# A two-layer decoder on one core: the 16-head weighted sums of its first and last stage on four quarters of the array, norms of the last stage by Ln and Exp, and new orders of both stages

## What is computed

```
x = x + L0_attn(ln(x))          # stage A: delta-rule attention, 4 heads of 32
x = x + L0_xattn(ln(x), ctx)    # stage B: causal attention on ctx, 16 heads of 8
x = x + L0_ffn(ln(x))           # stage C: 6 layers of local attention (16 heads of 64) and GELU MLP
x = x + L1_attn(ln(x))          # stage D: causal attention, q and k of unit length, 16 heads of 8
x = x + L1_xattn(ln(x), ctx)    # stage E: gated attention on ctx, 8 heads of 16
x = x + L1_ffn(ln(x))           # stage F: 16 experts, 3 chosen per token, all computed
```

## Time and profile before

| | us |
|---|---|
| median of 3 runs | 4253.59 (4252.46 to 4254.8) |
| the profiled execution's own time | 4263.92 |
| its span, first to last instruction | 4262.1 |
| TensorE busy | 4071.3 (96% of the span) |
| ScalarE busy | 3488.6 (82%) |
| VectorE busy | 3291.7 (77%) |
| GpSimd busy | 2653.4 (62%) |

### The profile page before, as it was taken

One profiled execution on the slowest core, in us unless ns is written; L12 is line 12 of the kernel. 1 busy time (PEld: TensorE's weight loads), 2 busy tenths in 40 slices (PEclk: granted clock), 3 DMA queues, 4 the chain that ended last, 5 costly groups with the idle time before them and its releaser, 6 DMA issues.

```text
span 4262.1 us, 149492 instructions
## 1 busy us (share of the span) xinstructions
PE 4071.3 (96%) x61520; PEld 3074.8 (72%) x61520; DVE 3291.7 (77%) x9529; ACT 3488.6 (82%) x10059; POOL 2653.4 (62%) x2246
## 2 busy tenths in 40 slices
PE   7999989999999999999999999999999799999999
PEld 5777756666667666667666666676666588888889
DVE  4666578998888888888888888888888467767765
ACT  3455569999999999999999999999999356666665
POOL 3444467887777777777777777777777233333331
PEclk8888889999999999999999999999999789999999
DMA  3000000000000000000000000000000100000000
GB/s 105 4 4 4 4 2 4 5 4 5 30 3 4 4 30 4 4 4 4 30 4 5 5 30 4 5 3 9 27 10 9 30 2 4 4 4 4 4 4 7
DMA packets 65248, 46.34 MB, mean 11 GB/s; under 512 B 29220, under 2 KB 63032, under 8 KB 63800
## 3 DMA queue, kind: packets, MB, share of 16 engines
q1 hardware_dynamic: 64568, 36.78, 3.0%
HBM read 28.48 MB, written 2.10 MB: 7 GB/s over the span
## 4 chain that ended last, share of the span: by engine, by line
PE 41%; ACT 34%; DVE 8%; issue 2%; POOL 0%; ACTq 0%
PE ps L569 34%; ACT BIG L921 15%; ACT BIG L913 12%; PE ps L573 7%; DVE BIG L1149 3%; ACT ps L913 3%; ACT L928 2%; DVE sm L1160 2%; DVE BIG L1154 1%; ACT sm L921 1%; DVE BIG L1157 1%; DVE y_sb L1154 0%; DVE BIG L1153 0%; ACT XS L913 0%; POOL BIG L1591 0%
## 5 line engine op out<-in xcount | busy, mean ns | idle before, releaser
L569 PE MATMUL ps<-WB,BIG 128*128 128x128 f32 (+2 forms) x8576 | 1940.8, 363 | 53.4 <-DVE BIG L1157 47.7
L913 ACT ACTIVATE BIG<-ps 128x512 f32<-128x512 f32 (+6 forms) x3168 | 1518.4, 536 | 461.6 <-PE ps L573 277.8
L1591 POOL TENSOR_TENSOR BIG<-BIG,sm 128x512 f32<-128x512 f32 (+1 forms) x864 | 1221.3, 1425 | 563.6 <-DVE sm L1342 330.0
L569 PEld LDWEIGHTS ps<-WB,BIG 128*128 128x128 f32 (+1 forms) x8576 | 1154.3, 192 | 378.8 <-issue 224.7
L1591 POOL TENSOR_TENSOR BIG<-BIG 128x512 f32<-128x512 f32 x768 | 969.4, 1279 | 146.5 <-DVE BIG L1149 146.5
L1160 DVE TENSOR_REDUCE sm<-BIG 128x8 f32<-128x512 f32 (+3 forms) x1472 | 871.3, 610 | 157.8 <-ACT BIG L921 154.6
L573 PEld LDWEIGHTS ps<-t_ident,BIG 128*128 128x128 f32 x6016 | 731.3, 146 | 325.8 <-issue 167.8
L573 PE MATMUL ps<-t_ident,BIG 128*128 128x128 f32 x6016 | 888.0, 282 | 68.3 <-DVE BIG L1149 28.9
L569 PEld LDWEIGHTS ps<-BIG 64*64 64x64 f32 (+2 forms) x37888 | 617.4, 132 | 336.6 <-ACT BIG L913 78.3
L569 PE MATMUL ps<-BIG 64*64 64x64 f32 (+4 forms) x37888 | 737.2, 226 | 52.7 <-ACT BIG L913 18.6
L1594 POOL TENSOR_TENSOR sm<-sm,halfn 128x1 f32<-128x1 f32 (+2 forms) x336 | 290.5, 871 | 752.0 <-DVE sm L1153 419.8
(11 more groups left out here) (119 smaller groups left out, 2913.7 us busy)
## 6 DMA issues: line engine op xcount, KB each, us to landing
WB<-in_Wqkv SPq DMA_DIRECT2D x6, 1536.0 KB, 7.3
XS<-y_sb SPq DMA_DIRECT2D x96, 63.0 KB
y_sb<-in_ctx SPq DMA_DIRECT2D x16, 256.0 KB, 3.2
WB<-in_Wo SPq DMA_DIRECT2D x6, 512.0 KB, 9.0
x_sb<-in_x SPq DMA_DIRECT2D x8, 256.0 KB, 5.2
WB<-in_F_W SPq DMA_DIRECT2D x1, 2048.0 KB, 8.7
WB<-in_F_W SPq DMA_DIRECT2D x8, 256.0 KB, 4.9
out<-x_sb SPq DMA_DIRECT2D x8, 256.0 KB, 2.3
```

Source lines behind the costliest of these rows:

```text
L569: return te.matmul(o, l, r, start=start, stop=stop, skip_group_check=not check)
L913: return se.activation(o, i, ACT.Copy)
L1591: return pe_.tensor_tensor(o, a, b, op)
```

## The change

1. `weighted16` goes over j = 0 to 7 and does heads j and 8 + j together. Heads 0 to 7 (n = 0) go to one bank on the two diagonal quarters, heads 8 to 15 (n = 1) to the next bank on the other two, so that four consecutive matmuls use the four quarters. The two sequences of heads 8 to 15 thus come out in exchanged rows. The number and the shapes of the matmuls are as before.
2. Phase `u` takes a pair of banks. DVE `r` and `n` read both in one instruction each (`weighted`).
3. ACT `t` puts the rows right (`restore`): three copies of 64x128, 64x64 and 64x64 in the place of one of 128x128.
4. In stage D, `n1` to `n8` go; ACT phases `ln` and `lx` of 128x32 come in (Ln, then Exp with scale -0.5), as stage C has them. `n0` becomes one `max`. The constant `magic` goes.
5. All lists of `AB_ORDER` and `DE_ORDER` are new, and so are `SLOT` and `BEGIN`. `C_ORDER` stays. Some conditions on the reuse of banks and buffers are written out (`act D` for G, `dve a` for J, `act h` beside `act k`), since the orders no longer imply them.

```
 AB_ORDER = {
-    "pe": "V3 b12 s4 O3 u5 a22 o3 b22 T1 w3 a32 b32 G1 a42 D1 b42 v4 x3 X0 p14 t5 q3 Z2 a11 W2 y5 p04 J0",
+    "pe": "X1 q4 y6 v5 W3 a12 J1 V3 s4 b12 p05 a22 O3 b22 u5 a32 T1 o3 b32 w3 G1 a42 D1 b42 t5 p14 x3 Z2",
...
-SLOT = {"ab": 14.8, "c": 11.25, "de": 25.4}
+SLOT = {"ab": 12.999, "c": 11.246, "de": 24.357}
 BEGIN = {
-    "ab": {"pe": -0.7, "act": -3.5, "dve": -10.8, "pool": -18.7},
-    "c": {"pe": 482.5, "act": 484.2, "dve": 473.3, "pool": 463.2},
-    "de": {"pe": 3239.8, "act": 3223.5, "dve": 3222.9, "pool": 3321.6},
+    "ab": {"pe": 0.0, "act": -19.09, "dve": -26.15, "pool": -23.17},
+    "c": {"pe": 428.13, "act": 426.37, "dve": 418.35, "pool": 408.78},
+    "de": {"pe": 3171.62, "act": 3143.0, "dve": 3143.34, "pool": 3118.64},
...
-AB_PAIRS = ("G", "s")
+AB_PAIRS = ("G", "s", "u")
...
-DE_PAIRS = ("s", "G")
+DE_PAIRS = ("s", "G", "u")
...
+        def weighted(u):
+
+            return PS[u.bank["u"] // 2][:, :].rearrange("p (n c) -> p n c", n=2)[:, :, 0:72].rearrange("p n (h d) -> p n h d", d=9)
...
-            def weighted16(K, PT, V):
-                for h in range(16):
-                    c = 128 * (h % 4) + 64 * (h // 4 % 2)
-                    for q in (slice(0, 64), slice(64, 128)):
-                        o = mm(K[q, 9 * h:9 * h + 9], PT[h // 8][q, c:c + 64], V[q, 9 * h:9 * h + 9])
+            def weighted16(k, PT, V):
+
+                for j in range(8):
+                    c = 128 * (j % 4) + 64 * (j // 4)
+                    for n in range(2):
+                        for bb in range(2):
+                            q, r, v = slice(64 * bb, 64 * bb + 64), slice(64 * (bb ^ n), 64 * (bb ^ n) + 64), 72 * n + 9 * j
+                            o = mm(bank[k + n][r, 9 * j:9 * j + 9], PT[n][q, c:c + 64], V[q, v:v + 9])
                 return o
...
+            def restore(o, K):
+
+                copy(o[0:64, :], K[0:64, 0:128])
+                copy(o[64:128, 0:64], K[64:128, 64:128])
+                return copy(o[64:128, 64:128], K[64:128, 0:64])
...
+                elif ph == "ln":
+                    w.wait_ge(*u.on("dve", "n0"))
+                    o = act(sm[:, 5, 0:32], sm[:, 2, 0:32], ACT.Ln)
+                elif ph == "lx":
+                    w.wait_ge(*u.on("act", "ln"))
+                    o = act(sm[:, 5, 0:32], sm[:, 5, 0:32], ACT.Exp, scale=-0.5)
...
-                    o = stt(sm[:, 2, 0:32], sm[:, 1, 0:32], 1e-16, sm[:, 1, 0:32], ALU.max, ALU.max)
-                elif ph[0] == "n" and len(ph) > 1:
-                    o = newton(u, sm[:, 5, 0:32], sm[:, 2, 0:32], sm[:, 6, 0:32], int(ph[1:]) - 1)
+                    o = ts(sm[:, 2, 0:32], sm[:, 1, 0:32], 1e-16, None, ALU.max)
```

More of the change, by code:

```diff
@@ L158 @@
 for _x in EXPERTS:
-    DE_EMPTIED.update({"h" + _x: ("act k" + _x,), "o" + _x: ("dve x" + _x,)})
-DE_PAIRS = ("s", "G")
+    DE_EMPTIED.update({"h" + _x: ("act h" + _x, "act k" + _x), "o" + _x: ("dve x" + _x,)})
+DE_PAIRS = ("s", "G", "u")
 class Unit:
@@ L239, in build @@
         halfn = sb("halfn", [128, 8])
-        magic = sb("magic", [128, 32], U32)
         woA = sb("woA", [128, 128])
@@ L674, in pe_ab @@
                         w.wait_ge(*u.on("act", m))
-                    o = weighted16(K, b.PT, b.V9)
+                    o = weighted16(u.bank[ph], b.PT, b.V9)
                 elif ph == "t":
@@ L899, in pe_de @@
                     w.wait_ge("wm2", 128)
+                    w.wait_ge(*u.on("act", "h" + ph[1]))
                     w.wait_ge(*u.on("act", "k" + ph[1]))
@@ L978, in act_ab @@
                 elif ph == "t":
-                    o = copy(b.OT, K[:, 0:128])
+                    o = restore(b.OT, K)
                 o.then_inc(u.name("act", ph, sems), 1)
@@ L1074, in act_de @@
                 t, b, sm = u.at["t"], de_bufs(u), de_bufs(u).sm
-                if ph in ("e0", "e1", "g1", "g2", "ex", "em", "x3"):
+                if ph in ("ln", "lx", "e0", "e1", "g1", "g2", "ex", "em", "x3"):
                     table("natural_log_exp_and_others")
@@ L1095, in act_de @@
                 elif ph == "t":
-                    o = copy(b.oT, K[:, 0:128])
+                    o = restore(b.oT, K)
                 elif ph == "xc":
@@ L1255, in dve_ab @@
                 elif ph == "r":
-                    o = ve.reciprocal(sm[:, 4, 0:16], K[:, 0:144].rearrange("p (h d) -> p h d", d=9)[:, :, 8])
+                    o = ve.reciprocal(sm[:, 4, 0:16].rearrange("p (n h) -> p n h", n=2), weighted(u)[:, :, :, 8])
                 elif ph == "n":
                     w.wait_ge(*u.on("dve", "r"))
-                    o = tt(b.On.rearrange("p (h d) -> p h d", d=8), K[:, 0:144].rearrange("p (h d) -> p h d", d=9)[:, :, 0:8],
-                           bc(sm[:, 4, 0:16], 8), ALU.mult)
+                    o = tt(b.On.rearrange("p (n h d) -> p n h d", n=2, d=8), weighted(u)[:, :, :, 0:8],
+                           sm[:, 4, 0:16].rearrange("p (n h) -> p n h", n=2).unsqueeze(3).broadcast_to([128, 2, 8, 8]), ALU.mult)
                 o.then_inc(u.name("dve", ph, sems), 1)
[L1263 to L1273, removed]
-                    return stt(t, t, -10.0 / 3.0, t, ALU.add, ALU.mult)
-                if i == 4:
-                    return stt(o, t, 5.0, o, ALU.add, ALU.mult)
-                if i == 5:
-                    return stt(t, o, -0.5 * (3.0 / 8.0) ** 3, a, ALU.mult, ALU.mult)
-                return stt(o, t, 1.5 * 3.0 / 8.0, o, ALU.add, ALU.mult)
             def dve_c1(u, ph):
@@ L1442, in dve_de @@
                     w.wait_ge(*u.on("dve", "ss"))
-                    o = stt(sm[:, 2, 0:32], sm[:, 1, 0:32], 1e-16, sm[:, 1, 0:32], ALU.max, ALU.max)
-                elif ph[0] == "n" and len(ph) > 1:
-                    o = newton(u, sm[:, 5, 0:32], sm[:, 2, 0:32], sm[:, 6, 0:32], int(ph[1:]) - 1)
+                    o = ts(sm[:, 2, 0:32], sm[:, 1, 0:32], 1e-16, None, ALU.max)
                 elif ph == "qn":
-                    w.wait_ge(*u.on("dve", "n8"))
+                    w.wait_ge(*u.on("act", "lx"))
                     o = tt(b.qn.rearrange("p (h d) -> p h d", d=8), b.qk.rearrange("p (h d) -> p h d", d=8), bc(sm[:, 5, 0:32], 8), ALU.mult)
@@ L1596, in _ @@
             pe_.memset(halfn[:, :], -0.5)
-            pe_.memset(magic[:, :], 0x5F3759DF)
             for p in range(4):
```

## The result

The changed kernel takes 4187.62 us (4180.02 to 4200.89, 4 runs) against 4253.35 us (4252.46 to 4254.8, 4 runs): ratio 0.9848, 95% interval 0.9834 to 0.9863. That is 65.7 us faster, inside the range given, but half of the 131 us that the sum had. The profiled execution took 4189.46 us.

A forecast was written before the change was run, and what follows sets the result against it. TensorE was taken to bound the first and last stages. First stage 88 us, last stage 38 and joints 5 summed to 131 us, putting the median at 4123 us from 4253.6, with a range of 4065 to 4195.

The forecast's parts named there:

- Burst `u`, 0.93 a tile in both stages: TensorE, first and last stage: four quarters shorten `u` from 1.95 to 1.02 us, all on the path, 58 us.
- two quarters or four: Rival, 8%: `u` stays at 1.95 us either way and the clock loss stays; 40 us gained, 4214 us.
- the rule on row groups: Skill text: weight loads overlap running matmuls only across row groups; by it `u` stays at 1.95 us, gaining nothing.
- Waits in the first stage, 0.85: TensorE, first stage: the new order cuts idle from 1.55 to about 0.7 us, 0.85 us less per tile.
- Clock in the first stage, 1.05: TensorE, first stage: rarer clock falls return two thirds of the 1.56 us lost per tile, 1.05 us.
- the first rival (20%): First stage: the clock gives nothing back, as other small bursts keep it low; 98 us gained, 4156 us; chance 20%.
- Last stage, 1.23 a tile: TensorE, last stage: 0.93 us from `u` and 0.3 from a shorter wait for VectorE's `C`; 38 us over 31 tiles.
- Joints +5: Between stages: 10 us of idle back, less 5 for four more table loads; the skill's estimate of 10.6 would leave nothing.
- Ln and Exp at nothing: Last stage: replacing eight VectorE steps (1.4 us a tile) by two ScalarE instructions gains and costs nothing.
- The pair of banks at nothing: Burst `u`: one bank more of eight in a slot costs nothing, as VectorE `n` empties it at once.
- Slower by a late `lx`: Rival, 5%: VectorE `qn` waits for ScalarE `lx` in the last stage; at 6 us a tile, 55 us slower, 4309 us.
- only shortens `u`: Rival, 4%: waits return elsewhere as long as before, and the clock loss too; 58 us gained, 4196 us.

The follow-up runs named there:

- run 3: The changed kernel with burst `u` put back on two quarters, new orders, norms, pair of banks and three copies kept: 4282.62 us, ratio 1.006.
- run 8: The changed kernel with the last stage's norm back on VectorE (eight root steps, no Ln and Exp): 4195.88 us, ratio 0.9861.
- run 4: The changed kernel with two unread 256-column matmuls on a 32x32 corner of the array in each first-stage `u`: 4214.77 us, ratio 0.9894.
- run 5: The changed kernel with two unread 256-column matmuls over the whole array in each first-stage `u`: 4173.41 us, ratio 0.9799.
- Run 6: The changed kernel with one unread 256-column matmul over the whole array in each first-stage `u`: 4177.4 us, ratio 0.9823.
- run 7: The kernel before with two unread 256-column matmuls over the whole array in each first-stage `u`: 4254.19 us, ratio 0.9993.
- run 10: The changed kernel with `T` moved ahead of `u` on TensorE and `K` ahead of `d2` on VectorE in the first stage: 4213.21 us, ratio 0.9894.
- run 11: The changed kernel with `T` ahead of `u`, `K` ahead of `d2`, and one unread whole-array matmul in first-stage `u`: 4211.08 us, ratio 0.9891.
- run 1: The kernel before with `u` on four quarters, its pair of banks and three copies, old orders and norms: 4354.59 us, ratio 1.0229.

## Why the prediction was right in sign and wrong by half

- **Burst `u`, 0.93 a tile in both stages: right.** 1.04 us to the next start in both. The row of the middle stage was the right one to take: with two quarters (run 3) it stays at 1.96. The rival "two quarters or four" is out, and so is what the prediction drew from the rule on row groups, that nothing was left to gain: the old and the new `u` alternate their rows alike, and differ by 0.9 us.
- **But all of it on the path: wrong in the first stage.** The pauses at the block ends, which I put down to code, give 26.1 - 1.0 = 25.1 us back; that is 0.81 of the 0.93 over 31 tiles, and 0.91 over the 27 above. "TensorE is the bound" was true of the queue as a whole; of what feeds it I had costed other engines and banks, and not its own code.
- **Waits in the first stage, 0.85: about right as waits, worth little as time.** The listed waits fell by 16.9 us over 410, some 0.65 a tile. Yet a full-clock tile without its pauses is only 1.01 shorter (1.16 in run 8), of which `u` is 0.91. The one at 331.87 shows it: idle is 0.53 us in place of 1.55, and busy 13.21 in place of 13.12 although `u` is 0.9 shorter. Other bursts take longer: `J` to its neighbour 341.44 - 340.43 = 1.01 us, where it was 141.38 - 140.63 = 0.75 (order of time on TensorE, kernel before, below). I can't split this 1 us further.

```profile
140.63 0.82 PE L569 MATMUL ps<-t_WA,BIG 128*128 128x388 f32 x2
141.38 2.32 PE L569 MATMUL ps<-BIG 32*32 32x32 f32 x80
```

- **Clock in the first stage, 1.05: the step that failed** together with the two above. It measured about 0.25 (0.46 in run 8), with 18 falls in place of 19, so the first rival (20%) nearly came true. I had read "19 of 20 falls behind a `u`" (18 of them within 2.5 us by a second count) as "the length of `u` brings them". Runs 4 to 7 show that it is what the array does there. That a `u` in half the time, with small bursts now packed on both sides of it, does not raise that is my reading; runs 10 and 11, meant to show it, did not.
- **Last stage, 1.23 a tile: right for the tile, short for the stage.** Full-clock tiles went from 26.3 or 27.0, mean 26.59, to 25.38, 1.21 less, and the wait for `C` from 40.4 to 27.0 us, 0.5 a tile where 0.3 was forecast. The other 21 of the 59 us came from what I had left out, in about equal parts: before, five tiles in the body of the stage hold a fall and take 28.7 us each, with the change none does (its 5 falls, of 11 before, all come in the first five tiles); and those first five tiles, where the stages overlap, take 17 us less together, where 1.21 each would be 6.
- **Joints +5: neither shown nor refuted.** The 4 us left over are of two single executions, and the changed kernel's four lie 21 us apart; they can't tell 5 from the 0 that the prediction's other estimate for the table loads gives. **Ln and Exp at nothing: right** as far as run 8 can tell. **The pair of banks at nothing: right only by the new order** (run 1).
- **Slower by a late `lx`: out.** Between 3400 and 4100 us VectorE's waits have none for ScalarE before `qn`, and run 8 without `lx` is no faster. Of the signs of being wrong only the second came, falls as frequent as before.

That the time lies in the range is luck in part. Without the 21 us of the last stage that no term had it would be 4209 us. And the upper end of 4195 is wider than what stands behind it: no clock gain and half the gain in waits leave 131 - 33 - 13 = 85 us, 4168. The rival "only shortens `u`" (4196 us) came nearest to the time, though not by its mechanism.

The best version here is run 5, 4173.41 us: the changed kernel with two useless matmuls over the whole array in each `u`. Run 6 can't be told from it.

## What to carry to other kernels

Where a bound engine's burst gets faster, ask what feeds it next: operands, banks, and its own code. When the clock falls behind a burst, change what the array does there before you believe that its duration is the cause; a full-array matmul of no use can pay for itself, but only if the place is otherwise not short of time (runs 5 and 7). And undo a change in halves: here each half, as run, was worth nothing or less, and only the two together gained.

## What the runs showed of the hardware

- Instruction fetches come as one packet of 16.4 KB for every 256 instructions of TensorE's queue (487 for 124,883). Where some 256 instructions run at 8 ns each, a pause of 0.3 to 1.9 us can stand at the block's end that no semaphore explains (28 of them in the changed kernel's first stage, 2 before).
- A busy TensorE does not hold the clock by being busy: 382 busy us of 400 at a clock of 0.84 with two matmuls on a corner of the array (run 4), 375 at 0.98 with two on the whole array (run 5).
- 32 products of 64x64 with 9 columns (64 instructions in the trace) take 1.95 us on two quarters of the array and 1.04 on four, with the halves of its rows alternating in both.
